# A decoder layer on one core: projections as a Strassen stage of their own, attention after it per head and batch

## The reference, cut to what matters

```
x = x + attn(layernorm(x))          # 32 query heads, 8 key/value heads, head size 128, rotary, causal
    q = h @ Wq   (1024 x 4096)      k = h @ Wk, v = h @ Wv   (1024 x 1024 each)
    out = softmax(q k^T / sqrt(128), causal) v ;  attn = out @ Wo   (4096 x 1024)
x = x + fake_quant(layernorm(x)) @ fake_quant(ctx)
x = x + ffn(layernorm(x))           # router over 64 experts of rank 8, 16 of them kept
```

## Time and profile before

| | us |
|---|---|
| median of 3 runs (1430.41 to 1435.37) | 1432.01 |
| span of the profiled execution | 1429.4 |
| PE busy | 1380.9 (97%) |
| DVE busy | 912.7 (64%) |
| ACT busy | 521.4 (36%) |
| POOL busy | 317.5 (22%) |

### The profile page before, as it was taken

The page is one execution under the profiler, slowest core; times in us unless marked ns, Lnnn a source line. Parts: engine busy times, 40 slices in busy tenths (PEclk is TensorE's granted clock), DMA queues, the critical chain, the costliest instruction groups (busy, mean ns, idle before and its releaser), DMA issues. The chain is left out here.

```text
span 1429.4 us, 20561 instructions
## 1 busy us (share of the span) xinstructions
PE 1380.9 (97%) x7185; PEld 1166.4 (82%) x7185; DVE 912.7 (64%) x2006; ACT 521.4 (36%) x1106; POOL 317.5 (22%) x178
## 2 busy tenths in 40 slices
PE   5999999999999999999999999999999999988998
PEld 4888878888888878887888878888888888857887
DVE  8598438853687349833884368634873389688753
ACT  4354214422343225412442144322441254256540
POOL 2232312222222312222223122231212222021100
PEclk9999999999999999999999999999999999999999
DMA  6110121003100221012110210021102205200001
GB/s 206 45 30 30 45 75 45 28 18 103 31 30 16 70 65 40 20 46 83 36 30 30 89 36 25 16 91 45 43 16 66 67 16 206 89 3 12 34 30 45
DMA packets 70394, 73.26 MB, mean 51 GB/s; under 512 B 2832, under 2 KB 51984, under 8 KB 70304
## 3 DMA queue, kind: packets, MB, share of 16 engines
q1 hardware_dynamic: 65696, 59.32, 13.0%
q10 hardware_dynamic: 4608, 12.58, 2.7%
HBM read 63.51 MB, written 8.39 MB: 50 GB/s over the span
## 5 line engine op out<-in xcount | busy, mean ns | idle before, releaser
L781 PE MATMUL banks<-xn_hi,ring_hi 128*128 128x512 f32 x768 | 305.1, 397 | 1.9 <-DVE xn_lo L550 1.9
L781 PE MATMUL banks<-xn_lo,ring_hi 128*128 128x512 f32 x768 | 300.7, 392 | 0.0
L781 PE MATMUL banks<-xn_hi,ring_lo 128*128 128x512 f32 x768 | 300.1, 391 | 0.0
L323 POOL TENSOR_TENSOR ring_lo<-raw,ring_hi 128x1024 fp32r<-128x1024 f32 x80 | 191.6, 2399 | 397.6 <-ACT ring_hi L410 397.6
L328 POOL TENSOR_TENSOR rope<-rope 128x512 f32<-128x512 f32 x80 | 103.4, 1292 | 535.9 <-DVE rope L594 535.9
L665 DVE TENSOR_TENSOR resid<-banks,resid 128x512 f32<-128x512 f32 x134 | 92.4, 690 | 192.2 <-PE banks L861 191.8
L861 PE MATMUL banks<-ring_hi,qo_hi 128*128 128x512 f32 x512 | 201.3, 393 | 1.3 <-DVE resid L665 1.2
L861 PE MATMUL banks<-ring_hi,qo_lo 128*128 128x512 f32 x512 | 199.5, 390 | 0.0
L861 PE MATMUL banks<-ring_lo,qo_hi 128*128 128x512 f32 x512 | 199.3, 389 | 0.0
L781 PEld LDWEIGHTS banks<-xn_hi,ring_lo 128*128 128x128 f32 x768 | 144.9, 189 | 31.1
L438 ACT CAST pT_hi<-banks 128x512 fp32r<-128x512 f32 (+1 forms) x192 | 86.4, 523 | 225.7 <-PE banks L819 225.7
(11 more groups left out here) (158 smaller groups left out, 2147.1 us busy)
## 6 DMA issues: line engine op xcount, KB each, us to landing
raw<-in_L_attn_Wq SPq DMA_DIRECT2D x32, 512.0 KB, 4.1
raw<-in_L_attn_Wo SPq DMA_DIRECT2D x32, 512.0 KB, 3.7
spare<-in_ctx ACTq DMA_DIRECT2D x16, 512.0 KB, 3.6
resid<-in_x SPq DMA_DIRECT2D x8, 512.0 KB, 7.3
raw<-in_L_attn_Wk SPq DMA_DIRECT2D x8, 512.0 KB, 3.6
raw<-in_L_attn_Wv SPq DMA_DIRECT2D x8, 512.0 KB, 3.6
q_dram<-cq ACTq DMA_DIRECT2D x16, 256.0 KB, 2.1
q<-q_dram SPq DMA_DIRECT2D x2, 2048.0 KB, 14.3
```

What stands on the lines that cost most here:

```text
L323: nc.gpsimd.tensor_tensor(ring[1][:, PLACE[name], :], raw[:, slot, :], as32(ring[0][:, PLACE[name], :]), ALU.subtract).then_inc(block_lo, 1)
L781: ins = nc.tensor.matmul(bank[par][:], ring[a][:, place, k * P:(k + 1) * P], xn[c][:, k, b * H:(b + 1) * H], start=(s == 0), stop=(s == 23))
```

## The change

The attention section is written anew. Nothing of it is a loop any more.

**Projections first.** Wq, Wk and Wv are cut into 12 panels of 512 output columns (s = 0, 1: k; 2 to 9: q; 10, 11: v). A panel's product with the input is a 2 by 2 block product: the input's two batches by two halves of the contraction, the weights' two halves of the contraction by two halves of the columns. It is done in Winograd's form of Strassen's method with seven block products, P1, P2, P6, P7, P4, P5, P3 in this order (`product`), where there were eight. Each block product is 2 column blocks (`fb`) of 12 matmuls of 512 columns, in the v panels 2 of 24 matmuls of 256 columns. The factors need sums: those of the input are made once (GpSimd and VectorE, `turn_sum` and `t3`) and all seven are turned and split (28 `fill`s of four transposes in place of 16); those of the weights are made by GpSimd in each panel (`weight_sum`: S1, S3, S2, S4). The results need sums too, which VectorE makes on the way out (`keep_u`, `c10`, `c11`, `c01`), together with the whole rotary embedding (`rope`, four instructions for a tile), and ScalarE keeps a copy of P1 (`keep_p1`). q, k and v are stored to DRAM in float32, 256 KB for a tile, through four staging places in `resid`; x is loaded a second time afterwards.

**Attention after it.** 64 units, one for each head and batch; half a group (one batch) is four units in a row. q is loaded, split and used per unit, k and v per four units. In a unit TensorE does the scores, one piece of Wo, the mix of the unit before, a second piece of Wo, and the turning of the probabilities. A piece is 12 matmuls of 512 columns as before; there are 128 in both kernels. Pieces begin with unit 5 (`pieces_of`), and ten are left behind the last unit. The quantised context stays on the chip.

```diff
-BODY = ["Q1", "Q2", "Q3", "Q0'", "K'", "V'", "A0", "A1", "B0", "B1"]
+PROD = ("P1", "P2", "P6", "P7", "P4", "P5", "P3")
+XI = {p: n for n, p in enumerate(PROD)}
+PANELS = 12
+ORDER = ([(0, "P1"), (0, "P2"), (1, "P1"), (1, "P2")] + [(s, p) for s in (0, 1) for p in PROD[2:]]
+         + [(s, p) for s in range(2, PANELS) for p in PROD])
+AT = {sp: n for n, sp in enumerate(ORDER)}
...
+        for n in range(4):
+            sp.wait_ge(st[n], 16 * (TILES // 4))
         for t in range(TT):
+            sp.dma_start(resid[:, t, :], x_t[t]).then_inc(x_in[t], 16)
+        for u in range(UNITS):
+            if u + 3 < UNITS:
+                load_q(u + 3)
+            if u % 4 == 0 and half_of(u) + 1 < HALVES:
+                load_kv(half_of(u) + 1)
+            for m in wo_after(u):
...
+        def w_low(n):
+            s, p = ORDER[n]
+            pool.wait_ge(w_hi, n + 1)
+            nc.gpsimd.tensor_tensor(wring[:, 1, n % 3, :], factor(s, p), as32(wring[:, 0, n % 3, :]),
+                                    ALU.subtract).then_inc(w_lo, 1)
+
+        def weight_sum(s, name):
+            use = 16 * (s // 2 + 1)
+            if name == "S1":
+                pool.wait_ge(w_in[s % 2][QUARTER["A10"]], use)
+                pool.wait_ge(w_in[s % 2][QUARTER["A11"]], use)
+                nc.gpsimd.tensor_tensor(ta[:], quarter(s, "A10"), quarter(s, "A11"), ALU.add).then_inc(w_sum, 1)
+            elif name == "S3":
+                nc.gpsimd.tensor_tensor(quarter(s, "A10"), quarter(s, "A00"), quarter(s, "A10"),
+                                        ALU.subtract).then_inc(w_sum, 1)
+            elif name == "S2":
+                pool.wait_ge(w_sum, 4 * s + SUMS["S3"])
+                nc.gpsimd.tensor_tensor(quarter(s, "A00"), ta[:], quarter(s, "A00"), ALU.subtract).then_inc(w_sum, 1)
+            else:
+                pool.wait_ge(w_sum, 4 * s + SUMS["S2"])
+                nc.gpsimd.tensor_tensor(quarter(s, "A01"), quarter(s, "A01"), quarter(s, "A00"),
+                                        ALU.subtract).then_inc(w_sum, 1)
...
+        def w_high(n):
+            s, p = ORDER[n]
+            if n >= 3:
+                act.wait_ge(p_done, 2 * (n - 3) + 2)
+            if p in ("P1", "P2", "P4"):
+                name = {"P1": "A00", "P2": "A01", "P4": "A11"}[p]
+                act.wait_ge(w_in[s % 2][QUARTER[name]], 16 * (s // 2 + 1))
+            else:
+                act.wait_ge(w_sum, 4 * s + SUMS[{"P6": "S2", "P7": "S3", "P5": "S1", "P3": "S4"}[p]])
+            nc.scalar.copy(wring[:, 0, n % 3, :], factor(s, p)).then_inc(w_hi, 1)
+
+        def keep_p1(s):
+            for fb in range(2):
+                act.wait_ge(p_done, done(s, "P1", fb))
+                nc.scalar.copy(p1_copy(s, fb), alpha(s, fb)).then_inc(p1_read, 1)
...
+        def rope(b, n):
+            turn = turns[n % 2]
+            if n >= 2:
+                dve.wait_ge(made, n - 1)
+            nc.vector.tensor_tensor(turn[0:64, :], b[64:128, :], sin[64:128, :], ALU.mult)
+            link(nc.vector.tensor_tensor(turn[64:128, :], b[0:64, :], sin[0:64, :], ALU.mult))
+            link(nc.vector.tensor_tensor(b, b, cos[:], ALU.mult))
+            slot_free(n)
+            nc.vector.tensor_tensor(qst[n % 4], b, turn, ALU.add).then_inc(made, 1)
...
+        def keep_u(s, which, fb):
+            dve.wait_ge(p_done, done(s, {2: "P6", 3: "P7"}[which], fb))
+            dve.wait_ge(p1_read, 2 * s + fb + 1)
+            if s >= 1:
+                dve.wait_ge(made, tile_no(s - 1, {2: "C01", 3: "C11"}[which], fb) + 1)
+            nc.vector.tensor_tensor(u_copy(which, fb), beta(fb), p1_copy(s, fb), ALU.add).then_inc(u_read, 1)
+
+        def c10(s, fb):
+            n = tile_no(s, "C10", fb)
+            dve.wait_ge(p_done, done(s, "P4", fb))
+            if s < 10:
+                link(nc.vector.tensor_tensor(beta(fb), beta(fb), p1_copy(s, fb), ALU.add))
+                rope(beta(fb), n)
+            else:
+                slot_free(n)
+                nc.vector.tensor_tensor(qst[n % 4], beta(fb), p1_copy(s, fb), ALU.add).then_inc(made, 1)
...
+        def c11(s):
+            for fb in range(2):
+                n = tile_no(s, "C11", fb)
+                dve.wait_ge(p_done, done(s, "P5", fb))
+                dve.wait_ge(u_read, 4 * s + 2 + fb + 1)
+                if s < 10:
+                    nc.vector.tensor_tensor(alpha(s, fb), gamma(fb), u_copy(3, fb), ALU.add).then_inc(c11_read, 1)
+                else:
+                    slot_free(n)
+                    nc.vector.tensor_tensor(qst[n % 4], gamma(fb), u_copy(3, fb), ALU.add).then_inc(c11_read, 1)
+                    dve.wait_ge(c11_read, 2 * s + fb + 1)
+                    dve.sem_inc(made, 1)
+            if s < 10:
+                for fb in range(2):
+                    dve.wait_ge(c11_read, 2 * s + fb + 1)
+                    rope(alpha(s, fb), tile_no(s, "C11", fb))
...
-        def project(par, name, b, n, steps=range(24)):
-
-            place = PLACE[name]
-            for s in steps:
-                k, (a, c) = s // 3, PASSES[s % 3]
-                if s == 0:
-                    if b == 0:
-                        pe.wait_ge(block_lo, n + 1)
-                ins = nc.tensor.matmul(bank[par][:], ring[a][:, place, k * P:(k + 1) * P],
-                                       xn[c][:, k, b * H:(b + 1) * H], start=(s == 0), stop=(s == 23))
-                if s == 23:
-                    ins.then_inc(piece_done, 1)
...
+        def product(s, p, fbs=(0, 1)):
+            n = AT[s, p]
+            opens = p in ("P1", "P6", "P5")
+            for fb in fbs:
+                if fb == 0:
+                    pe.wait_ge(w_lo, n + 1)
+                    if s == 0:
+                        pe.wait_ge(fill_lo, FILLED[p])
+                if p == "P1" and s >= 2:
+                    pe.wait_ge(made, tile_no(s - 2, "C11", fb) + 1)
+                elif p == "P2":
+                    pe.wait_ge(p1_read, 2 * s + fb + 1)
+                elif p == "P6" and s >= 1:
+                    pe.wait_ge(made, tile_no(s - 1, "C10", fb) + 1)
+                elif p == "P7":
+                    pe.wait_ge(u_read, 4 * s + fb + 1)
+                elif p == "P4":
+                    pe.wait_ge(u_read, 4 * s + 2 + fb + 1)
+                elif p == "P5" and s >= 1:
+                    pe.wait_ge(made, tile_no(s - 1, "C01", fb) + 1)
+                elif p == "P3":
+                    pe.wait_ge(c11_read, 2 * s + fb + 1)
+                dst = product_bank(s, p, fb)
+                for tt in ((None,) if s < 10 else (2 * fb, 2 * fb + 1)):
+                    for k in range(KH):
+                        for i, (a, c) in enumerate(PASSES):
+                            first = opens and k == 0 and i == 0
+                            if tt is None:
+                                ins = nc.tensor.matmul(dst, wring[:, a, n % 3, k * 256 + fb * P:k * 256 + (fb + 1) * P],
+                                                       xc[:, XI[p], c, k, :], start=first,
+                                                       stop=(k == KH - 1 and i == 2), skip_group_check=True)
+                            else:
+                                ins = nc.tensor.matmul(dst[:, (tt % 2) * 256:(tt % 2) * 256 + 256],
+                                                       xc[:, XI[p], a, k, tt * P:(tt + 1) * P],
+                                                       wring[:, c, n % 3, k * 256:(k + 1) * 256],
+                                                       start=first and tt % 2 == 0,
+                                                       stop=(k == KH - 1 and i == 2), skip_group_check=True)
+                ins.then_inc(p_done, 1)
...
+            for k in range(HPG):
+                for p, (a, c) in enumerate(PASSES):
+                    ins = nc.tensor.matmul(bank[n % 2], oT[a][:, h % 2, k, t * P:(t + 1) * P],
+                                           wo[c][:, 2 * half + k // 2, (k % 2) * 512:(k % 2) * 512 + 512],
+                                           start=(k == 0 and p == 0), stop=(k == HPG - 1 and p == 2))
+            ins.then_inc(piece_done, 1)
...
-        with pe.Fori(0, GROUPS - 1) as g:
-            body(g, False)
-        body(GROUPS - 1, True)
...
+        fills(range(8))
+        product(0, "P1")
+        product(0, "P2")
+        fills(range(8, 12))
+        product(1, "P1")
+        fills(range(12, 16))
...
+        product(0, "P6", (0,))
+        fills(range(24, 26))
+        product(0, "P6", (1,))
+        fills(range(26, 28))
+        for s, p in ORDER[5:]:
+            product(s, p)
+
+        for u in range(UNITS):
+            scores(u)
+            for n in pieces_of(u)[:1]:
+                piece(n)
+            if u > 0:
+                mix(u - 1)
+            for n in pieces_of(u)[1:]:
+                piece(n)
+            turn_probs(u)
+        piece(PIECES - 10)
+        mix(UNITS - 1)
+        for n in range(PIECES - 9, PIECES):
+            piece(n)
```

(28 more changed lines are left out.)

1167 lines of the change are left out of this document (553 added, 614 removed).

## The result

| us | before | after |
|---|---|---|
| median (lowest to highest, 4 runs each) | 1433.36 (1430.41 to 1435.37) | 1389.24 (1388.67 to 1391.34) |
| span of the profiled execution | 1429.4 | 1387.4 |

The ratio is 0.9704, with an interval of 0.9681 to 0.9726: faster by 42 us in the two profiled executions, where 47.4 were forecast. The first matmul of L1478 on the normalised rows, behind the attention, starts at 1237.8 where its counterpart L1376 started at 1279.9. That is 42.1 earlier, so the whole difference lies ahead of it.

A forecast was written before the change was run, and what follows sets the result against it. TensorE was taken as the bound. The terms summed to -47.4 us, bringing the span from 1429.4 to 1382.0; with the median 2.6 above it the forecast was 1385 us, range 1362 to 1415.

The forecast's parts named there:

- 1, projections: q, k, v products: 2304 matmuls replaced by 1680 and 672 of 256 columns at 0.123 us each; -58.3 us.
- 3, the loop: Attention loop's head: six places of 4.0 us, waits and the lower clock behind them, go; -24 us, ends -13 and -27.
- 4, the opening: First five attention units, without pieces: TensorE idles and the clock falls; +25 us, ends +15 and +42.
- 5, the lock: Units 8g + 6, seven of them: VectorE's scaling held by GpSimd's subtractions, 0.75 us each; +5 us, between 0 and 12.
- 6, two tight chains: k and q panels: chains P4 to P3 and P5 to P2 hardly fit beside TensorE's matmuls; +2 us, ends 0 and +10.
- 7, the start: Before the panels: fills wait for GpSimd's 1024-column instructions and VectorE's layernorm and input differences; +3 us, ends 0 and +8.
- A gap of more than 8 us in the start: Sign in the kernel's start: a gap of this size would make the prediction wrong.
- 7, the end: At the end, four tiles' statistics on VectorE stand ahead of an addition that a piece waits for; +1.5 us.
- 8, transfers: q, k, v out and in, and the queue behind x at the attention's start: held hidden, but for item 4's high end.
- the chains don't fit: Rival, k and q panels: each microsecond a chain is late counts ten times; +20 us, 1405; chance 0.13.
- VectorE sets the panels by the lock: Rival, k and q panels: GpSimd holds VectorE's instructions with one SBUF operand too; +74 us, 1459; chance 0.06.
- The opening costs its high end: Rival, attention's first five units: the queue behind x and the clock cost +17 us more, 1402; chance 0.12.

The follow-up runs named there:

- Experiment 3: Changed kernel with P7's 24 matmuls issued twice in the ten k and q panels: 1444.19 us, ratio 1.0068 to the kernel before.
- experiment 1: Kernel before with its seven loop rounds written out one behind the other, nothing else changed: 1410.37 us, ratio 0.9832.
- experiment 4: Changed kernel with twelve additional matmuls, results unused, behind the mix in attention units 0 to 4: 1390.39 us, ratio 0.9696 to the kernel before.
- experiment 9: Changed kernel with TensorE's wait for the mixed output's low part moved behind the first two of three chunks of turnings: 1382.60 us, ratio 0.9652.
- experiment 7: Changed kernel with the first C11 sum of each k and q panel made three times on VectorE: 1405.44 us, ratio 0.9808.
- experiment 6: Changed kernel with GpSimd's third weight sum in the start waiting until VectorE has scaled the layernorm's second half: 1390.70 us, ratio 0.9713.
- experiment 8: Changed kernel with x's second load issued behind the transfers of attention unit 0, no longer ahead: 1390.11 us, ratio 0.9703.
- experiment 5: Changed kernel with GpSimd's third weight sum in the start waiting for the layernorm's second-half row statistics: 1392.84 us, ratio 0.9724.

## Why the prediction was right, point by point

The forecast of 1385 is 4 us below the 1389.24 measured, inside the likeliest case's own 1374 to 1397. The traces show the mechanism of every large item but the start's, which the forecast named only in part. That the sum came so near is partly luck: the start cost 11 us more than forecast, and five other items together cost about 5 less. By its items:

- **1, projections, -58.3.** No wait in the panels. In v, 40 matmuls of 256 columns start at 505.73, and the next matmul at 510.53:

```profile
505.73 4.96 PE L958 MATMUL banks<-wring,xc 128*128 128x256 f32 x40
510.53 0.40 PE L978 MATMUL banks<-kT_hi,q_hi 128*128 128x512 f32 x1
```

  That is 0.120 us each, not 0.123: 2 us more gain. The 0.140 from the scores is ruled out for this stage; the nearest row was the right choice. An estimate of 109 ns had been worked out from the Trainium skill (TensorE: Matmul & The Clock Gate, section Back-to-back issue gap), whose formula is for a single matmul by itself; these 40 (0.120) do not agree with it. Experiment 3 shows that every matmul in the panels of k and q stands on the path.
- **3, the loop, -24.** -24.1 by experiment 1. Its waits alone (13) would have been too little; the lower clock behind them is the rest.
- **4, the opening, +25.** Idle 18.45 where the items came to 19.6, said as 20 (unit 0 4.41 for 4.2; units 1, 3, 4 2.22, 2.23, 2.95 for 3.2; unit 2 6.64 for 5.7). The whole stretch from 510.53 to 566.90 is 56.4 us for 31.7 of work at full clock (six scores of 2.00, five mixes of 1.85, five turnings of 1.01, 24 matmuls of a unit's pieces at 0.226), so 24.7 lost. The sum is right. The clock's 5 was too much for the path: about 3.3 by experiment 4's units, of which that experiment itself recovers 1.2.
- **5, the lock, +5.** 4.4, by the very mechanism: scaling of 2.88 us, end at 9.8 behind the turning, the low part behind an addition, 0.7 us a unit for 0.75. There are six such units and not seven: unit 62 has no k and v of a next half to split. The trace of the new kernel agrees here with the Trainium skill (SBUF — State Buffer, section Who interferes with whom), and experiment 9 takes the price away without touching the lock.
- **6, two tight chains, +2.** 0, with a room of 0.13 us in the first (experiment 7). GpSimd's sums over 1024 columns are 2.40, not the 2.58 that I had doubled from a 512-column row: twice the half costs more than the whole. By the forecast's own sum that gives the second chain 0.36 us more room; no run measured that room.
- **7, the start, +3.** This is the step that failed in size. The gaps between the first turning and panel 2 are 15.0 us. With the slower matmuls at the lower clock and the restarts, counted by how far each matmul's start is from the next, less the median of its shape, 22.4 us are lost there; the old kernel loses 8.4 in its first 110 us (gaps 5.3). So the change costs about 14. The text named the mechanism, the lock on operands that are all in SBUF, and put its high end at 8. It missed two things. The lock also holds instructions of four elements (the gap of 4.2 us at 35.19; experiment 6 takes it away and is 3.0 us ahead up to panel 0's last products). And the rotary work and additions of VectorE, which fit into one panel, do not fit where panels 0 and 1 overlap: `ORDER` puts both panels' P1 and P2 ahead, so that TensorE reaches panel 1's P7 two products behind panel 0's last, while VectorE has panel 0's quarters to finish first (7.3 at 100.83). I had compared sums per panel, and looked for chains only in the steady panels. "A gap of more than 8 us in the start" would have made the prediction wrong; the largest was 7.3.
- **7, the end, +1.5.** One wait of 2.5 on L809 where before had 1.2 and 0.4: +0.9.
- **8, transfers.** Hidden but for waits of ScalarE in unit 2, 0.92 and 0.93; they came from the queue behind x, and taking them away brought nothing that the runs can tell (experiment 8).

With -58.3 - 2.0 - 1.6 - 24.1 + 24.7 + 4.4 + 0.9 + 14 the sum is -42.0, as measured. No term is better than to half a microsecond or so, so that it comes out to the tenth is chance.

Of the rivals, "the chains don't fit" falls for this kernel, since no wait for them is in the list, but it holds as a warning: with 0.13 us of room, one more VectorE instruction of 0.73 in each panel's first chain would cost about 10 x 0.6 us, by experiment 7. "VectorE sets the panels by the lock" falls with L720 and L738, which lie between 680 and 700 ns. "The opening costs its high end" falls with the 24.7 us of item 4.

## What to carry to other kernels

Fewer products pay in full only where TensorE has no gap; count each helping engine's work not only per steady round but at the seams, where two rounds overlap, and look there at the order of its queue. A wait should stand before the instruction that needs it and not at the head of the group: moving one by eight transposes gave 6.6 us. And judge a small edit by the distances inside its own stage: in these runs the total moved by 1 to 3 us with stretches of the lower clock that the edit had nothing to do with. And a hardware loop's head can cost as much as the algorithm on top of it gains: here 24 of 42 us.

## What was not expected of the hardware

- The lock reaches the smallest instructions: a tensor_tensor of four elements a partition took 1.97 and 2.26 us beside GpSimd, 0.16 when GpSimd stood still (experiment 5).
- Holding GpSimd back by one short wait moved the lock onto the next instruction of its kind: 5.70 us for two scalings that take 1.54.
- The same program runs at more than one mean clock: in experiment 6 1385.5 us at 0.990, and 1390.6 to 1392.1 at 0.984 to 0.985. A gain of 3 us in front of such a place could not be told from none by its median.
- Behind one and the same wait of 2.5 us the clock stayed up in three profiled executions of the changed kernel and its variants and fell in seven, which then took 1.0 to 1.4 us more.
